# A gate and a depthwise convolution on one core: one product for four taps, other places for the small products, another split of the rows

## Chip, cores and metric

The kernel runs on one core of one Trainium2 chip. The metric is the time on the device in microseconds (us) for one execution; the median of the runs is taken.

## The reference, cut to what matters

The input x has 32 images of 96 channels of 56 x 56 pixels, in fp32. A first layer makes, from image 0, a choice of a 7 x 7 cosine basis for each channel; each image is averaged to 7 x 7 cells, weighted by the basis, mixed over the channels, and gives a gain y. The second layer takes a gain-scaled image, its mean over the pixels, a hidden layer of 24 units, and from it the weights of a depthwise 3 x 3 convolution. The mask keeps four taps: left-up, up, right-up and left.

```
x  = x * y[:, :, None, None] + x                 # y: relu of the mixed, weighted cell means
t  = relu(gamma * (mean(x) @ w1.T - m) * rsqrt(v + eps) + beta)      # 24 units
wt = (t @ w2.T + b2) * MASK                      # 4 live taps per channel
out = depthwise_conv3x3(x, wt) + bias
```

The gain is a factor of each image and channel, so the kernel folds it into the taps, and convolves the x that it loaded.

## The kernel before, in words

The 3,072 planes (image x channel) are 24 tiles of 128 partitions with one plane of 56 x 56 each; three tiles (t = 0, 1, 2) are a group of four images, and there are eight groups g. The taps of a group depend on the cell sums of its own three tiles, so sums run ahead: while tile k is convolved, GpSimd (POOL) folds tile k + 6 in three halvings (`fold_once`, `fold_twice`, `fold_thrice`, L402, L407, L412), and VectorE (DVE) sums the cells of tile k + 5 (`sum_ahead`, L533).

The rows of a tile are split by `ROWS` into three parts, in tiles 0 to 17: 27 rows are D, 18 rows are B, 11 rows are A.
- **A** is the array's part: ScalarE (ACT) seeds a PSUM accumulator with the tap "up" and the bias (`seed_a`), TensorE (PE) adds the other three taps with diagonal matrices in two chunks of rows (`array_taps`), ACT copies it out (`finish_array`, L761).
- **B** is mixed: ACT seeds it (`seed_b`), PE adds two taps in two chunks (`mixed_taps`), DVE adds the last on the way out (`finish_mixed`, L652).
- **D** is DVE's: ACT seeds it (`seed_d`), DVE adds three taps in three instructions (`tap`, L643: LEFT_UP, RIGHT_UP, then LEFT, which writes the result and counts `d_out`).

Every fp32 matmul of the program shows twice in the trace. The accumulators of A, B and D are single: `seed_b` of tile k waits for `finish_mixed` of tile k - 1, `seed_d` waits for LEFT of tile k - 1. The last six tiles (18 to 23, `tail`) have another split with a fourth part for POOL and ACT (`part_rows`, `part`).

Column 0 of D and B has no left neighbours. POOL computes it apart in three instructions (L457, L460, L462) at the start of its step for tile k, before the folds.

Taps of the next group come from a chain of small steps woven into the current group:
1. DVE, tile t = 0: `weigh_cells` (L549, L552, L555) gives `by_image`.
2. PE, tile t = 1: `mix` (L828, L830, twelve records) between the two chunks of A.
3. ACT: `lift_relu` (L706), behind `seed_b` of t = 1, or in the last tiles behind `part`.
4. DVE: `total_step` (L562), between LEFT_UP and RIGHT_UP of t = 1.
5. PE: `hide` (L836) between the chunks of B; ACT: `hidden_relu` (L711), behind `finish_array`; PE: `make_taps` (L842), four products, one for each tap.
6. DVE, tile t = 2: `gained_step` (L567) behind LEFT_UP; PE: `spread_taps` (L849) ahead of B; DVE: `coef_steps` (L574, L579), behind RIGHT_UP.
7. ACT: `diagonals` (L717) and all seeds of t = 0 need the new coefficients.

Each engine has one queue, worked in the order written. SyncE issues all large transfers, nine input and four output buffers: for tile k it waits for B and the edge column, loads tile k + 9, waits for D and A, and stores tile k.

Of the kernel before, what the change touches and what calls it, by code (L numbers as in the profile page):

```python
# [33 lines left out]
ROWS = (27, 18, 11, 0)  # L34
# [84 lines left out]
def build(nc, x, early, narrow, wide, out):  # L119
# [9 lines left out]
    with ExitStack() as ctx:  # L129
# [13 lines left out]
        gate_in = sb("gate_in", [P, E_HID - E_GATE2])  # L143
# [9 lines left out]
        hidden = sb("hidden", [HID, GROUP])  # L153
# [8 lines left out]
        rs_hid = sb("rs_hid", [HID, 1])  # L162
# [4 lines left out]
        a_hid = sb("a_hid", [HID, 1])  # L167
        b_hid = sb("b_hid", [HID, 1])
# [14 lines left out]
        hid_par = early_sb[0:HID, E_HID - E_GATE2:E_END - E_GATE2]  # L183
# [37 lines left out]
        p_hidden = small[0:HID, S_HIDDEN:S_TAPS]  # L221
# [85 lines left out]
        lift_done = sem("lift_done")  # L307
        total_done = sem("total_done")
# [24 lines left out]
        edge_begun = sem("edge_begun")  # L333
        edge_out = sem("edge_out")
# [5 lines left out]
        def _(sp):  # L340
# [22 lines left out]
            for k in range(TILES - 1):  # L363
                sp.wait_ge(b_out, k + 1)
                sp.wait_ge(edge_out, k + 1)
                if k + IN_BUFS < TILES:
                    load(k + IN_BUFS).then_inc(loaded[k % IN_BUFS], 16)
# [21 lines left out]
        def _(pool):  # L389
            eng = nc.gpsimd  # L390
            eng.memset(gate_w[:, :, :], 0.0).then_inc(gate_zeroed, 1)
            eng.memset(expo[:, :], -0.5).then_inc(expo_set, 1)
            pool.wait_ge(expo_set, 1)
# [3 lines left out]
            eng.tensor_tensor(rs_hid[:, :], b_hid[:, :], expo[0:HID, 0:1], ALU.pow).then_inc(rsqrt_done, 1)  # L397
# [49 lines left out]

            for k in range(TILES):
                pool.wait_ge(coef_done, k // PER + 1)
                pool.wait_ge(pad_zeroed, 1)  # L450
                if k >= OUT_BUFS:
                    pool.wait_ge(stored[k % OUT_BUFS], 16 * (k // OUT_BUFS))
                pool.wait_ge(loaded[k % IN_BUFS], 16 * (k // IN_BUFS + 1))
                n = top_a(k)
                rows = grid(k)[:, 0:n, 0:2]
                each = coef[:, k // PER % 2, k % PER, UP:RIGHT_UP + 1].rearrange("p (r c) -> p r c", r=1)
                eng.tensor_tensor(edges[:, 0:2, 0:n].rearrange("p c r -> p r c"), rows, each.broadcast_to([P, n, 2]),  # L457
                                  ALU.mult).then_inc(edge_begun, 1)
# [5 lines left out]
                if tail(k):  # L464
                    part_rows(k)
# [218 lines left out]
        def _(act):  # L684
# [85 lines left out]
            for k in range(TILES):  # L770
                g, t = k // PER, k % PER
                seed_b(k)
                if tail(k):
                    part(k)
                if t == 1 and g + 1 < NGROUP:
                    lift_relu(g + 1)
# [198 lines left out]
```

## Time and profile before

| what | value |
|---|---|
| median of 3 runs | 220.35 us (218.67 to 220.83) |
| the profiled execution's own time | 220.57 us |
| its span, first to last instruction | 218.5 us |
| TensorE | 196.0 us busy, 90% |
| VectorE | 193.4 us busy, 89% |
| ScalarE | 134.8 us busy, 62% |
| GpSimd | 172.6 us busy, 79% |
| the chain that ended last | PE 47%, DVE 34%, ACT 7% |

Busy shares are means over a start (to about 36 us), a steady stretch and a tail (from about 173 us). The chain that ended last follows each instruction back to what released it.

### The profile page before, as it was taken

Reading aid. Unit: us, or ns where it says so; the run is one execution under the profiler, and the core shown is the slowest. Engines: PE = TensorE matmul, PEld = TensorE weight load, DVE = VectorE, ACT = ScalarE, POOL = GpSimd, SP = SyncE. Lnnn points to the kernel's source line nnn. Section 1 sums busy time; section 2 is a strip of 40 time slices with the busy share of each in tenths; the row PEclk is TensorE's granted clock in tenths of the full one; section 3 lists DMA queues with packets and bytes.
Section 4 is the critical chain, followed back from the end, with each engine's and each line's share of the span. In section 5 each row is a group of like instructions: output and inputs, shape, how many; then the busy total and the mean of one; then the engine's idle time right before and its main releaser. Section 6 shows DMA issues by size and latency. Waiting matters only on the chain.

```text
span 218.5 us, 2505 instructions
## 1 busy us (share of the span) xinstructions
PE 196.0 (90%) x742; PEld 120.5 (55%) x742; DVE 193.4 (89%) x223; ACT 134.8 (62%) x208; POOL 172.6 (79%) x169
## 2 busy tenths in 40 slices
PE   7382875999999999999999999999999999899990
PEld 3041464675666566657655764675556656665550
DVE  6137958999999999999999999999999997989992
ACT  2001115367585768576867687577658796989960
POOL 4005149799999999999999999999999996696870
PEclk9888555899999999999999999999999999999999
DMA  4999999939999999999999999999999475446677
GB/s 104 262 429 402 441 427 432 417 111 344 425 413 395 413 418 420 427 423 423 430 425 423 439 425 425 430 434 417 432 432 386 188 298 220 184 184 294 294 293 296
DMA packets 8157, 79.07 MB, mean 362 GB/s; under 512 B 1040, under 2 KB 1072, under 8 KB 2128
## 3 DMA queue, kind: packets, MB, share of 16 engines
q1 hardware_dynamic: 8144, 78.92, 88.3%
q8 instruction: 5, 0.08, 0.1%
q14 instruction: 8, 0.07, 0.1%
HBM read 40.38 MB, written 38.54 MB: 361 GB/s over the span
## 4 chain that ended last, share of the span: by engine, by line
PE 47%; DVE 34%; ACT 7%; issue 5%; DMA 3%; SPq 1%; DVEq 1%; ACTq 0%
PE banks L857 33%; DVE banks L643 17%; DVE xout L643 7%; ACT banks L722 4%; DVE xout L652 3%; DMA xout<-x 3%; PE banks L805 3%; PE banks L842 2%; PE banks L828 2%; PE banks L849 2%; PE banks L830 2%; PE banks L792 1%; DVE stats L533 1%; DVE sums L552 1%; DVE stats L520 1%
## 5 line engine op out<-in xcount | busy, mean ns | idle before, releaser
L857 PE MATMUL banks<-xin,diag 128*128 128x330 f32 (+4 forms) x480 | 158.7, 483 | 2.8 <-ACT banks L722 2.7
L857 PEld LDWEIGHTS banks<-xin,diag 128*128 128x128 f32 x480 | 89.2, 193 | 54.8 <-issue 36.3
L722 ACT ACTIVATE banks<-xin,wide_sb,coef 128x616 f32<-128x616 f32 (+4 forms) x77 | 84.8, 1119 | 17.0 <-DVE xout L652 10.2
L402 POOL TENSOR_TENSOR halves<-xin 128x1568 f32<-128x1568 f32 (+2 forms) x22 | 74.0, 3368 | 22.9 <-DVE count L592 13.6
L643 DVE SCALAR_TENSOR_TENSOR banks<-xin,coef,banks 128x1485 f32<-128x1485 f32 (+2 forms) x48 | 82.9, 1727 | 1.6 <-ACT banks L722 0.4
L643 DVE SCALAR_TENSOR_TENSOR xout<-xin,coef,banks 128x1485 f32<-128x1485 f32 (+4 forms) x31 | 42.1, 1377 | 0.9 <-issue 0.3
L407 POOL TENSOR_TENSOR halves<-halves 128x784 f32<-128x784 f32 x18 | 33.3, 1849 | 1.4
L652 DVE SCALAR_TENSOR_TENSOR xout<-xin,coef,banks 128x990 f32<-128x990 f32 (+1 forms) x24 | 29.1, 1212 | 1.7 <-PE banks L857 1.6
L717 ACT ACTIVATE diag<-wide_sb,coef 128x128 f32<-128x128 f32 x72 | 23.4, 389 | 10.5 <-DVE coef L579 10.5
L761 ACT ACTIVATE xout<-banks 128x616 f32<-128x616 f32 (+2 forms) x24 | 15.8, 656 | 15.4 <-PE banks L857 14.8
L412 POOL TENSOR_TENSOR rows<-halves 128x392 f32<-128x392 f32 x18 | 18.3, 1017 | 1.4
L520 DVE TENSOR_REDUCE stats<-xin 128x14 f32<-128x896 f32 (+3 forms) x9 | 11.0, 1227 | 7.8 <-DMA xin<-x 7.8
L533 DVE TENSOR_REDUCE stats<-rows 128x49 f32<-128x392 f32 x18 | 10.0, 555 | 0.0
L439 POOL TENSOR_TENSOR xout<-xout,halves 128x385 f32<-128x385 f32 (+1 forms) x6 | 5.4, 908 | 5.6 <-ACT xout L722 5.6
L842 PEld LDWEIGHTS banks<-hidden,narrow_sb 32*96 32x96 f32 x64 | 6.6, 173 | 5.5 <-issue 5.0
L691 ACT ACTIVATE banks<-banks,b_gate,a_gate 128x784 f32<-128x784 f32 x1 | 1.0, 977 | 13.7 <-PE banks L805 13.7
L435 POOL TENSOR_TENSOR halves<-xin,coef 128x385 f32<-128x385 f32 (+1 forms) x12 | 9.3, 798 | 0.0
L805 PE MATMUL banks<-xout,gate_w 128*128 128x392 f32 x12 | 5.7, 637 | 3.7 <-DMA xout<-x 3.7
L457 POOL TENSOR_TENSOR edges<-xin,coef 128x90 f32<-128x90 f32 (+2 forms) x24 | 8.4, 348 | 0.0
L828 PEld LDWEIGHTS banks<-by_image,wide_sb 128*96 128x96 f32 x48 | 5.2, 178 | 5.5 <-DVE by_image L555 4.1
L460 POOL TENSOR_TENSOR edges<-edges 128x45 f32<-128x45 f32 (+2 forms) x24 | 6.7, 277 | 1.9
L849 PEld LDWEIGHTS banks<-taps,wide_sb 96*128 96x128 f32 x48 | 7.0, 208 | 1.9 <-ACT banks L722 1.0
(79 smaller groups left out, 115.1 us busy)
## 6 DMA issues: line engine op xcount, KB each, us to landing
xin<-x SPq DMA_DIRECT2D x23, 1568.0 KB, 10.4
out<-xout SPq DMA_DIRECT2D x23, 1568.0 KB, 12.6
xout<-x SPq DMA_DIRECT2D x4, 294.0 KB, 5.2
xin<-x SPq DMA_DIRECT2D x1, 1120.0 KB, 14.7
out<-xout SPq DMA_DIRECT2D x1, 700.0 KB, 3.3
wide_sb<-wide SPq DMA_DIRECT2D x1, 499.5 KB, 16.0
xin<-x SPq DMA_DIRECT2D x1, 448.0 KB, 15.3
out<-xout SPq DMA_DIRECT2D x1, 448.0 KB, 3.4
```

What stands on the lines that cost most here:

```text
L402: eng.tensor_tensor(halves[:, j % 2, 0:end, :], cells[:, :, 0, :], cells[:, :, 1, :], ALU.add).then_inc(once_folded, 1)
L407: eng.tensor_tensor(cells[:, :, 0, :], cells[:, :, 0, :], cells[:, :, 1, :], ALU.add).then_inc(twice_folded, 1)
L412: eng.tensor_tensor(rows8[:, j % 2, :].rearrange("p (a f) -> p a f", a=DCT), cells[:, :, 0, :], cells[:, :, 1, :], ALU.add).then_inc(thric ...
L520: return vec.tensor_reduce(cells_of(j, first, end), xin[:, j % IN_BUFS, PAD + first * BLK * W:PAD + end * BLK * W].rearrange("p (a b c d) ...
L533: return vec.tensor_reduce(stats[:, 0, j % PER, :], rows8[:, j % 2, :].rearrange("p (c d) -> p c d", d=BLK), AX.X, ALU.add)
L643: return vec.scalar_tensor_tensor(out=to, in0=grid(k)[:, irows, cols], scalar=weight(k, which), in1=acc, op0=ALU.mult, op1=ALU.add)
L652: vec.scalar_tensor_tensor(out=result(k)[:, top_b(k):top_a(k), ocols], in0=grid(k)[:, irows, cols], scalar=weight(k, LEFT), in1=acc_b(k).r ...
L717: ins = sca.activation(diag[:, k % 2, which, :], ident, ACT.Copy, scale=weight(k, which))
L722: return sca.activation(acc, above_rows(k, first, end), ACT.Identity, bias=bias[:, k % PER:k % PER + 1], scale=weight(k, UP))
L761: sca.activation(xout[:, k % OUT_BUFS, top_a(k) * W:top_p(k) * W], acc_a(k), ACT.Copy).then_inc(a_out, 1)
L805: ins = mm(gate_out[:, part], gate_w[:, t, :], image0[:, t, part], start=(t == 0), stop=(t == PER - 1))
L857: return mm(to, diag[:, k % 2, which, :], grid(k)[:, irows, cols], start=False, stop=(which == LEFT), skip_group_check=True)
```

## The change

- `ROWS` is 27/17/12 in place of 27/18/11: one row of each of tiles 0 to 17 goes from B to A.
- The hidden layer's product has its weights four times side by side, so its 32 rows appear in four blocks of partitions. `hidden_relu` is four instructions, one for each block, into a block-diagonal tile zeroed once, and `make_taps` is one product over 128 rows in place of four over 32. Parameters of the hidden layer are laid on 128 partitions; five copies on ScalarE at the start make the wider weights.
- ScalarE's order: `lift_relu` stands ahead of `part`, `hidden_relu` behind `diagonals`.
- `mix` stands behind the second chunk of A.
- In tiles 0 to 17 the edge column is two instructions on ScalarE (`edge_products`, behind `seed_b` and `lift_relu`) and one on POOL (`edge_sum`, behind the folds). The last six tiles keep POOL's three. The load of tile k + 9 waits for ScalarE's two and not for the edge column's end.

The sizes of `gate_in`, `rs_hid`, `a_hid`, `b_hid`, `p_hidden`, new semaphores and the zeroing of `hidden` on POOL are left out of the diff.

```diff
@@ -31,7 +31,7 @@
 
 
 
-ROWS = (27, 18, 11, 0)
+ROWS = (27, 17, 12, 0)
 TAIL_ROWS = (24, 16, 9, 7)
 LAST_ROWS = (25, 16, 10, 5)
 AHEAD_FOLD = 6
...
@@ -150,7 +150,9 @@
         by_image = sb("by_image", [P, 2, PER, GROUP])
         lift = sb("lift", [C, GROUP])
         total = sb("total", [C, GROUP])
-        hidden = sb("hidden", [HID, GROUP])
+        hidden = sb("hidden", [P, TAPS, GROUP])
+        w_hid4 = sb("w_hid4", [C, TAPS, HID])
+        w_tap4 = sb("w_tap4", [P, C])
         taps = sb("taps", [C, TAPS, GROUP])
         spread = sb("spread", [P, PER * TAPS, GROUP])
         coef = sb("coef", [P, 2, PER, TAPS])
...
@@ -362,9 +368,10 @@
 
             for k in range(TILES - 1):
                 sp.wait_ge(b_out, k + 1)
+                if k + IN_BUFS < TILES:
+                    sp.wait_ge(edge_scaled, 2 * k + 2)
+                    load(k + IN_BUFS).then_inc(loaded[k % IN_BUFS], 16)
                 sp.wait_ge(edge_out, k + 1)
-                if k + IN_BUFS < TILES:
-                    load(k + IN_BUFS).then_inc(loaded[k % IN_BUFS], 16)
                 sp.wait_ge(d_out, k + 1)
                 sp.wait_ge(a_out, k + 1)
                 if tail(k):
...
@@ -445,23 +453,35 @@
                 pool.wait_ge(part_step, 2 * n + 2)
                 eng.tensor_tensor(to, to, scaled, ALU.add).then_inc(part_out, 1)
 
+            def edge_rows(k):
+
+                pool.wait_ge(coef_done, k // PER + 1)
+                pool.wait_ge(edge_out, k)
+                pool.wait_ge(pad_zeroed, 1)
+                pool.wait_ge(stored[k % OUT_BUFS], 16 * (k // OUT_BUFS))
+                pool.wait_ge(loaded[k % IN_BUFS], 16 * (k // IN_BUFS + 1))
+                m = top_a(k)
+                n = k - (TILES - AHEAD_FOLD)
+                rows = grid(k)[:, 0:m, 0:2]
+                each = coef[:, k // PER % 2, k % PER, UP:RIGHT_UP + 1].rearrange("p (r c) -> p r c", r=1)
+                eng.tensor_tensor(edges[:, 0:2, 0:m].rearrange("p c r -> p r c"), rows, each.broadcast_to([P, m, 2]),
+                                  ALU.mult).then_inc(edge_begun, 1)
+                pool.wait_ge(edge_begun, 2 * n + 1)
+                eng.tensor_tensor(edges[:, 2, 0:m], edges[:, 0, 0:m], edges[:, 1, 0:m], ALU.add).then_inc(edge_begun, 1)
+                pool.wait_ge(edge_begun, 2 * n + 2)
+                eng.tensor_tensor(result(k)[:, 0:m, 0], edges[:, 2, 0:m],
+                                  bias[:, k % PER:k % PER + 1].broadcast_to([P, m]), ALU.add).then_inc(edge_out, 1)
+
+            def edge_sum(k):
+
+                n = top_a(k)
+                pool.wait_ge(edge_scaled, 2 * k + 2)
+                eng.tensor_tensor(result(k)[:, 0:n, 0], result(k)[:, 0:n, 0], edges[:, k % 2, 0:n],
+                                  ALU.add).then_inc(edge_out, 1)
+
             for k in range(TILES):
-                pool.wait_ge(coef_done, k // PER + 1)
-                pool.wait_ge(pad_zeroed, 1)
-                if k >= OUT_BUFS:
-                    pool.wait_ge(stored[k % OUT_BUFS], 16 * (k // OUT_BUFS))
-                pool.wait_ge(loaded[k % IN_BUFS], 16 * (k // IN_BUFS + 1))
-                n = top_a(k)
-                rows = grid(k)[:, 0:n, 0:2]
-                each = coef[:, k // PER % 2, k % PER, UP:RIGHT_UP + 1].rearrange("p (r c) -> p r c", r=1)
-                eng.tensor_tensor(edges[:, 0:2, 0:n].rearrange("p c r -> p r c"), rows, each.broadcast_to([P, n, 2]),
-                                  ALU.mult).then_inc(edge_begun, 1)
-                pool.wait_ge(edge_begun, 2 * k + 1)
-                eng.tensor_tensor(edges[:, 2, 0:n], edges[:, 0, 0:n], edges[:, 1, 0:n], ALU.add).then_inc(edge_begun, 1)
-                pool.wait_ge(edge_begun, 2 * k + 2)
-                eng.tensor_tensor(result(k)[:, 0:n, 0], edges[:, 2, 0:n],
-                                  bias[:, k % PER:k % PER + 1].broadcast_to([P, n]), ALU.add).then_inc(edge_out, 1)
                 if tail(k):
+                    edge_rows(k)
                     part_rows(k)
                 j = k + AHEAD + 1
                 if j < TILES:
@@ -472,6 +492,8 @@
                     fold_twice(j)
                     pool.wait_ge(twice_folded, j - AHEAD)
                     fold_thrice(j)
+                if not tail(k):
+                    edge_sum(k)
 
 
         @block.vector
...
@@ -693,6 +715,9 @@
             act.wait_ge(gate2_mm, 1)
             sca.activation(gate_act[:, :], p_gate2, ACT.Tanh, bias=gate_par[0:NF, 4:5],
                            scale=1.0 / HW).then_inc(gate_tanh, 1)
+            act.wait_ge(narrow_in, 16)
+            for which in range(TAPS):
+                sca.activation(w_tap4[HID * which:HID * (which + 1), :], w_tap[:, which, :], ACT.Copy).then_inc(w_tap_copied, 1)
             act.wait_ge(chosen_done, 1)
             sca.activation(chosen_rows[:, :, :, :],
                            chosen[:, :, :].rearrange("p t (j q) -> p t j q", j=1).broadcast_to([NF, PER, GROUP, QUAD]),
@@ -700,6 +725,9 @@
             act.wait_ge(wide_in, 16)
             act.wait_ge(filt_mm, 1)
             sca.activation(p_mask, image_of, ACT.Copy).then_inc(mask_set, 1)
+            sca.activation(w_hid4[:, :, :], w_hid.rearrange("p (k h) -> p k h", k=1).broadcast_to([C, TAPS, HID]),
+                           ACT.Copy).then_inc(w_hid_copied, 1)
+            act.wait_ge(hidden_zeroed, 1)
 
             def lift_relu(g):
                 act.wait_ge(total_mm, g + 1)
@@ -708,8 +736,10 @@
 
             def hidden_relu(g):
                 act.wait_ge(hidden_mm, g + 1)
-                sca.activation(hidden[:, :], p_hidden, ACT.Relu, bias=b_hid[:, :],
-                               scale=a_hid[:, :]).then_inc(hidden_done, 1)
+                for which in range(TAPS):
+                    rows = slice(HID * which, HID * (which + 1))
+                    sca.activation(hidden[rows, which, :], p_hidden[rows, :], ACT.Relu, bias=b_hid[rows, :],
+                                   scale=a_hid[rows, :]).then_inc(hidden_done, 1)
 
             def diagonals(k):
                 act.wait_ge(coef_done, k // PER + 1)
@@ -721,6 +751,18 @@
                 act.wait_ge(loaded[k % IN_BUFS], 16 * (k // IN_BUFS + 1))
                 return sca.activation(acc, above_rows(k, first, end), ACT.Identity, bias=bias[:, k % PER:k % PER + 1],
                                       scale=weight(k, UP))
+
+            def edge_products(k):
+
+                n = top_a(k)
+                if k >= OUT_BUFS:
+                    act.wait_ge(stored[k % OUT_BUFS], 16 * (k // OUT_BUFS))
+                sca.activation(result(k)[:, 0:n, 0], grid(k)[:, 0:n, 0], ACT.Identity,
+                               bias=bias[:, k % PER:k % PER + 1], scale=weight(k, UP)).then_inc(edge_scaled, 1)
+                if k >= 2:
+                    act.wait_ge(edge_out, k - 1)
+                sca.activation(edges[:, k % 2, 0:n], grid(k)[:, 0:n, 1], ACT.Copy,
+                               scale=weight(k, RIGHT_UP)).then_inc(edge_scaled, 1)
 
             def seed_a(k):
                 if k > 0:
@@ -770,15 +812,18 @@
             for k in range(TILES):
                 g, t = k // PER, k % PER
                 seed_b(k)
+                if t == 1 and g + 1 < NGROUP:
+                    lift_relu(g + 1)
                 if tail(k):
                     part(k)
-                if t == 1 and g + 1 < NGROUP:
-                    lift_relu(g + 1)
+                else:
+                    edge_products(k)
                 finish_array(k)
+                if k + 1 < TILES:
+                    diagonals(k + 1)
                 if t == 1 and g + 1 < NGROUP:
                     hidden_relu(g + 1)
                 if k + 1 < TILES:
-                    diagonals(k + 1)
                     seed_a(k + 1)
                     seed_d(k + 1)
 
@@ -833,14 +878,18 @@
             def hide(g):
 
                 pe.wait_ge(total_done, g + 1)
-                mm(p_hidden, w_hid, total[:, :], start=True, stop=True).then_inc(hidden_mm, 1)
+                if g == 0:
+                    pe.wait_ge(w_hid_copied, 1)
+                mm(p_hidden, w_hid4[:, :, :].rearrange("p k h -> p (k h)"), total[:, :],
+                   start=True, stop=True).then_inc(hidden_mm, 1)
 
             def make_taps(g):
 
-                pe.wait_ge(hidden_done, g + 1)
-                for which in range(TAPS):
-                    ins = mm(p_taps[:, which, :], w_tap[:, which, :], hidden[:, :], start=True, stop=True)
-                ins.then_inc(taps_mm, 1)
+                if g == 0:
+                    pe.wait_ge(w_tap_copied, TAPS)
+                pe.wait_ge(hidden_done, TAPS * (g + 1))
+                mm(p_taps.rearrange("p k n -> p (k n)"), w_tap4[:, :], hidden[:, :, :].rearrange("p k n -> p (k n)"),
+                   start=True, stop=True).then_inc(taps_mm, 1)
 
             def spread_taps(g):
 
@@ -880,9 +929,9 @@
                 pe.wait_ge(diag_done, k + 1)
                 pe.wait_ge(seeded_a, k + 1)
                 array_taps(k, 0)
+                array_taps(k, 1).then_inc(conv_a, 1)
                 if t == 1 and ahead:
                     mix(g + 1)
-                array_taps(k, 1).then_inc(conv_a, 1)
                 pe.wait_ge(seeded_b, k + 1)
                 if t == 2 and ahead:
                     spread_taps(g + 1)
```

## Rows read from the trace of the kernel before

**Rows 1.** Windows by engine, one steady group: length, busy us (instructions), clock, DMA share, GB/s.
```profile
105.80:128.30 22.50, 22.40 (x89) 13.69 (x88) 21.92 (x23) 15.96 (x24) 21.56 (x19) 1.00 1.01 429
```
**Rows 2.** Timeline, VectorE: start us, length us, engine, line, operation, count, idle before.
```profile
101.15 0.16 DVE L567 SCALAR_TENSOR_TENSOR taps<-lift,banks 96x16 f32<-96x16 f32 x1
...
103.19 0.20 DVE L579 TENSOR_REDUCE coef<-spread 128x12 f32<-128x48 f32 x1
...
105.79 1.25 DVE L652 SCALAR_TENSOR_TENSOR xout<-xin,coef,banks 128x990 f32<-128x990 f32 x1 [0.26 <-PE banks L857]
...
113.66 0.18 DVE L555 TENSOR_TENSOR by_image<-sums,banks 128x24 f32<-128x24 f32 x1
...
116.58 0.15 DVE L562 SCALAR_TENSOR_TENSOR total<-lift,banks 96x4 f32<-96x4 f32 x1
...
118.52 1.76 DVE L643 SCALAR_TENSOR_TENSOR xout<-xin,coef,banks 128x1485 f32<-128x1485 f32 x1
...
121.98 1.77 DVE L643 SCALAR_TENSOR_TENSOR banks<-xin,coef,banks 128x1485 f32<-128x1485 f32 x1
...
123.65 0.16 DVE L567 SCALAR_TENSOR_TENSOR taps<-lift,banks 96x16 f32<-96x16 f32 x1
```
**Rows 3.** The same timeline, TensorE's products.
```profile
101.60 0.74 PE L849 MATMUL banks<-taps,wide_sb 96*128 96x16 f32 x6
...
102.19 11.61 PE L857 MATMUL banks<-xin,diag 128*128 128x495 f32 x34
...
113.89 0.67 PE L828 MATMUL banks<-by_image,wide_sb 128*96 128x4 f32 x6
...
114.42 0.65 PE L830 MATMUL banks<-by_image,wide_sb 128*96 128x4 f32 x6
...
118.16 0.22 PE L836 MATMUL banks<-total,wide_sb 96*32 96x4 f32 x2
...
120.17 0.84 PE L842 MATMUL banks<-hidden,narrow_sb 32*96 32x4 f32 x8
```
**Rows 4.** The same timeline, ScalarE.
```profile
104.32 2.40 ACT L722 ACTIVATE banks<-xin,wide_sb,coef 128x616 f32<-128x616 f32 x2
...
116.16 0.34 ACT L706 ACTIVATE lift<-banks,b_chan,a_chan 96x4 f32<-96x4 f32 x1
...
116.61 0.68 ACT L761 ACTIVATE xout<-banks 128x616 f32<-128x616 f32 x1
...
118.42 0.35 ACT L711 ACTIVATE hidden<-banks,b_hid,a_hid 32x4 f32<-32x4 f32 x1 [1.13 <-PE banks L836]
...
118.68 0.97 ACT L717 ACTIVATE diag<-wide_sb,coef 128x128 f32<-128x128 f32 x3
...
119.56 3.58 ACT L722 ACTIVATE banks<-xin,wide_sb,coef 128x616 f32<-128x616 f32 x3
```
**Rows 5.** Timeline of POOL, two of its instructions.
```profile
106.44 0.35 POOL L457 TENSOR_TENSOR edges<-xin,coef 128x90 f32<-128x90 f32 x1
...
107.45 3.54 POOL L402 TENSOR_TENSOR halves<-xin 128x1568 f32<-128x1568 f32 x1
```
**Rows 6.** Timelines of PE and DVE, the first group's chain.
```profile
46.46 0.59 PE L828 MATMUL banks<-by_image,wide_sb 128*96 128x4 f32 x6
...
48.70 0.15 DVE L562 SCALAR_TENSOR_TENSOR total<-lift,banks 96x4 f32<-96x4 f32 x1
...
54.47 1.77 DVE L643 SCALAR_TENSOR_TENSOR banks<-xin,coef,banks 128x1485 f32<-128x1485 f32 x1 [0.44 <-ACT banks L722]
```
**Rows 7.** Timelines of ACT and DVE, the last group's chain.
```profile
184.57 0.57 ACT L761 ACTIVATE xout<-banks 128x504 f32<-128x504 f32 x1
185.27 0.35 ACT L711 ACTIVATE hidden<-banks,b_hid,a_hid 32x4 f32<-32x4 f32 x1
...
188.14 2.14 ACT L722 ACTIVATE banks<-xin,wide_sb,coef 128x840 f32<-128x840 f32 x2 [0.21 <-DVE xout L643]
...
184.70 0.15 DVE L562 SCALAR_TENSOR_TENSOR total<-lift,banks 96x4 f32<-96x4 f32 x1 [1.04 <-ACT lift L706]
```

More of the change, by code:

```diff
@@ L142, in build @@
         gate_w = sb("gate_w", [P, PER, P])
-        gate_in = sb("gate_in", [P, E_HID - E_GATE2])
+        gate_in = sb("gate_in", [P, E_END - E_GATE2])
         early_sb = sb("early_sb", [C, E_END - E_GATE2])
@@ L161, in build @@
         rs_gate = sb("rs_gate", [P, 1])
-        rs_hid = sb("rs_hid", [HID, 1])
+        rs_hid = sb("rs_hid", [P, 1])
         a_chan = sb("a_chan", [C, 1])
@@ L166, in build @@
         b_gate = sb("b_gate", [P, 1])
-        a_hid = sb("a_hid", [HID, 1])
-        b_hid = sb("b_hid", [HID, 1])
+        a_hid = sb("a_hid", [P, 1])
+        b_hid = sb("b_hid", [P, 1])
         gate_sum = sb("gate_sum", [P, 1])
@@ L182, in build @@
         chan_par = early_sb[:, E_CHAN - E_GATE2:E_GATE - E_GATE2]
-        hid_par = early_sb[0:HID, E_HID - E_GATE2:E_END - E_GATE2]
+        hid_par = gate_in[:, E_HID - E_GATE2:E_END - E_GATE2]
         ones = narrow_sb[:, N_ONES:N_SHIFT]
@@ L220, in build @@
         p_total = small[0:C, S_TOTAL:S_HIDDEN]
-        p_hidden = small[0:HID, S_HIDDEN:S_TAPS]
+        p_hidden = small[:, S_HIDDEN:S_TAPS]
         p_taps = small[0:C, S_TAPS:S_SPREAD].rearrange("p (k n) -> p k n", k=TAPS)
@@ L307, in build @@
         lift_done = sem("lift_done")
+        w_hid_copied = sem("w_hid_copied")
+        w_tap_copied = sem("w_tap_copied")
+        hidden_zeroed = sem("hidden_zeroed")
         total_done = sem("total_done")
@@ L333, in build @@
         edge_begun = sem("edge_begun")
+        edge_scaled = sem("edge_scaled")
         edge_out = sem("edge_out")
@@ L392, in _ @@
             eng.memset(expo[:, :], -0.5).then_inc(expo_set, 1)
+            eng.memset(hidden[:, :, :], 0.0).then_inc(hidden_zeroed, 1)
             pool.wait_ge(expo_set, 1)
@@ L396, in _ @@
             eng.tensor_tensor(rs_chan[:, :], b_chan[:, :], expo[0:C, :], ALU.pow).then_inc(rsqrt_done, 1)
-            eng.tensor_tensor(rs_hid[:, :], b_hid[:, :], expo[0:HID, 0:1], ALU.pow).then_inc(rsqrt_done, 1)
+            eng.tensor_tensor(rs_hid[:, :], b_hid[:, :], expo[:, 0:1], ALU.pow).then_inc(rsqrt_done, 1)
             def fold_once(j, end=DCT):
@@ L484, in _ @@
             for j in range(GROUP):
-                vec.tensor_copy(gate_in[QUAD * j:QUAD * (j + 1), :], early_sb[0:NF, 0:E_HID - E_GATE2]).then_inc(gate_copied, 1)
+                vec.tensor_copy(gate_in[QUAD * j:QUAD * (j + 1), :], early_sb[0:NF, :]).then_inc(gate_copied, 1)
             vec.tensor_scalar(b_chan[:, :], chan_par[:, 4:5], EPS, None, ALU.add).then_inc(fold, 1)
+            dve.wait_ge(gate_copied, GROUP)
             vec.tensor_scalar(b_hid[:, :], hid_par[:, 3:4], EPS, None, ALU.add).then_inc(fold, 1)
-            dve.wait_ge(gate_copied, GROUP)
             vec.tensor_scalar(b_gate[:, :], gate_par[:, 3:4], EPS, None, ALU.add).then_inc(fold, 1)
```

## The prediction, made before the changed kernel ran

> **What bounds the kernel now.** I read the page's busy shares, then windows over single groups of three tiles, then the timeline of one group engine by engine, then the waits. The steady stretch repeats every 22.50 us, and in it three engines and the transfers are nearly full: PE 22.40, DVE 21.92, POOL 21.56 us, DMA share 1.01 at 429 GB/s; only ACT (15.96) has room [rows 1]. The reader is to see that nobody has a large wait, so what counts is the cycle of hand-overs in which one group's taps are made. Let G be the end of `gained_step`, 101.31 (101.15 and 0.16) [rows 2]. PE then spreads the taps and works 34 records without a gap (B of t=2, A and B of t=0, the first chunk of A of t=1) until 113.80, and `mix` starts at 113.89, 0.05 after `by_image` ends at 113.84 [rows 2, 3]. `mix` ends at 115.07. ACT takes the lift at 116.16, because `seed_b` held it, and DVE starts `total_step` at 116.58, directly behind its tap. So between the end of `mix` and the lift there is 1.09 us of slack, and DVE waits for nothing there [rows 2 to 4]. DVE's only wait in a group is 0.26 us, for PE, ahead of `finish_mixed` of t=2 [rows 2]. Its own work would thus make 22.24.
>
> **Rows 27/17/12.** B has two taps on PE, A three. Per tile PE has 2 x (4 x 495 + 3 x 330 + 3 x 275) = 7,590 columns, afterwards 2 x (2 x 495 + 2 x 440 + 6 x 330) = 7,700. The block of 34 records has 13,530 columns in 11.61 us, 0.858 ns each [rows 3]; 110 more are 0.09 us a tile, 0.28 a group. DVE's `finish_mixed` loses 55 of 990 elements, 0.06 us a tile. At t=2, though, the first tap waits for `seed_d` and not for `finish_mixed`: it starts at 121.98, 1.70 after LEFT ended at 120.28, which is ACT's `seed_d` (about 1.6) and two hand-overs [rows 2, 4]. There the 0.06 is worth nothing.
>
> **One product for four taps.** `make_taps` takes 0.77 of PE (120.17 to the next product at 120.94) and becomes one pair, about 0.20 like a pair of `spread_taps` (0.59 for three pairs). `hide` has 128 columns of weights for 32, some 0.05 more [rows 3]. PE's own work falls to 22.40 + 0.28 - 0.57 + 0.05 = 22.16 a group. But both products stand behind `mix`, in a part of the cycle where PE isn't last. The price is on ACT: `hidden_relu` is four instructions. One occupies ACT for 0.26 (118.42 to 118.68) [rows 4]. The trace has no such followers; they lie between 0.19 (a diagonal takes 0.29 and has 128 columns, 0.11 us at the seeds' pace) and 0.35 (its whole length). I take 0.25, nearest to the row of the same shape.
>
> **Mix behind A's second chunk.** This is the costly step. From G: spreading starts 0.05 later, now that PE comes earlier (it was 0.29), and takes 0.59: G+0.64. B of t=2, 3,740 columns, 3.21: 3.85. A of t=0 needs its seed: coefficients end at G+2.08 and `seed_a` started at G+3.01 [rows 2, 4]; with 0.85 and 0.06 for its new row it ends at 3.92, and A starts at 3.96. A, B and now both chunks of A, 11,660 columns, 10.00: 13.96. Then 0.09 and `mix` 1.18: 15.23. Lift 0.05 and 0.34, hand-over 0.08: `total_step` starts at G+15.70. Before it started at G+15.27. DVE, which has shed its 0.26 wait and 0.06, now stands idle there, and behind it wait RIGHT_UP, LEFT, the sum, `finish_mixed` and the next `gained_step`: 7.23 us that nothing shortens. The cycle becomes 22.9, and I take **0.40 us more a group**. Bounds: without the late seed and at 0.833 ns a column (two cycles at the granted 1.00, 2.4 GHz) 0.2; above, with a late ScalarE, 0.8 (below).
>
> **Edges, and the order on ScalarE.** POOL gives up 1.01 us a tile (106.44 to 107.45) [rows 5] and gets back one instruction of 0.3 and a gap. Nothing waited for POOL: its edge column is ready at 107.45, and the store that needs it waits for the tile's B, one tile later, so this is worth nothing. Moved behind the folds it ends about 6.5 us later, still some 2.5 us ahead of B's end. SyncE's queue is not delayed: load of k+9 waits for ACT's two, done while B is still in the array. ACT gains 0.5 us a tile. It has 6.5 us idle in a group [rows 1], most of it at t=0 and t=2, where it waits for A, LEFT and the coefficients; that covers four of the six. At t=1, between lift and `seed_d`, it now has lift 0.25, edges 0.50, copy 0.68, diagonals 0.88, hidden 1.00, `seed_a` 0.86: 4.17 behind a lift at G+15.28, so 19.45; DVE's LEFT ends at 15.70 + 3.70 = 19.40 and a hand-over later `seed_d` could start. Just in time, without reserve. If the cover is gone, every 0.05 us on the six small instructions is 0.3 us a group.
>
> **Start and tail.** In the first group `mix` starts at 46.46 with PE behind [rows 6]; 2,090 more columns make 1.79 us, and `total_step` comes at 49.87 for 48.70. Of these 1.17 us the 0.44 that the next tile waited for ACT takes up its part: +0.8. Ahead of it, four hidden instructions (+0.7) and a shorter `make_taps` (-0.9 at the low clock) cancel. The new copies lie in ACT's idle time. In the last group DVE waited 1.04 us for a lift behind `part` [rows 7]; that goes. But ACT ran full from there to `seed_d` with 0.21 idle: three more hidden instructions (0.75) meet 0.21 and a pause of 0.2 ahead of the hidden one, so the next tile starts 0.2 to 0.4 later all the same. I take +0.2.
>
> **Sum.** 0.8 + 5 x 0.40 + 0.2 = +3.0 us. The profiled execution, 220.57 with a span of 218.5, would become 223.6, its span 221.5; it lies 0.2 above the median of 220.35, so **223.4** for the median.
>
> **Rivals.**
> - *DVE sets the pace* (not slower). If PE came to the end of `mix` 0.6 us earlier than I reckon, `total_step` would not wait and DVE's own cycle decides: 22.50 less 0.12 (the 0.26 wait, of which `seed_d` of t=0 gives back the rest) and 0.06 = 22.32. For it: PE sheds 0.24 a group. Against: that is shed behind `mix`, and PE waits for `gained_step`, so it can't be carried on. The point: `mix` ended by G+14.7. Price -0.9 over five groups, the tail near zero: 219.4; with all of the 1.04 kept, 218.4. The transfers allow it, barely: 429 GB/s now [rows 1]. The Trainium skill, "DMA: Bandwidth & Descriptors", section "Where 436 GB/s comes from", puts the ceiling of the ports at 435.2 GB/s, which for 9.63 MB is 22.13 us a group. By that rule no engine's relief is worth over 0.4 us a group, or about 218; the trace agrees in that no steady window shows more than 429.
> - *The chunk costs half* (within 1%). Seeds on time and small hand-overs: 0.2 a group, 0.6 at the start: +1.7, 222.0.
> - *ScalarE late as well* (slower still). Small instructions at 0.30: seven of them add 0.35, `seed_d` of t=2 is late: 0.75 a group, tail 0.5: +5.0, 225.4.
> - That POOL's relief or the combined product does not come about would change nothing, as neither is on the cycle.
>
> **Chances.** Forecast's case 0.50 (222.6 to 224.3), ScalarE late 0.12, half cost 0.22, DVE's pace 0.16. About 1%, 2.2 us, is what a measurement here can tell from no change. Slower by over 1% takes the first two: 0.62. Within 1% has the half cost and most of DVE's pace: 0.31; faster 0.07, where the tail's 1.04 is kept too. Range 220.3 to 225.0: it leaves out most of DVE's pace and the upper part of the late ScalarE.
>
> **What would show it.** `total_step` with an idle time of 0.4 to 0.6 us released by ACT's lift in each steady group; `finish_mixed` without its wait; TensorE waiting for `gained_step` ahead of spreading; groups 22.9 apart; POOL with some 0.6 us idle a tile; ACT without idle time between lift and `seed_d` of t=1. I am wrong if groups are under 22.5 apart, or if DVE's longest wait is for `seed_d`.

## The result, and the profile after

The changed kernel takes 227.12 us (median of 4 runs, 226.25 to 228.42) beside 220.59 for the kernel before: 1.031 times, 95% interval 1.027 to 1.036. The forecast was 223.4 with a range to 225.0. The direction was right and the amount was half of what came. Medians here and below are over all executions, while the ratios leave out those that ran over 1.5% above the fastest of their kernel, at a lower granted clock, so the two need not have the same order. The profiled execution has a span of 224.2 us, 5.7 more than before.

Busy times of two groups, each from one `gained_step` to the next. Columns are length, busy us with instructions for PE, PE's weight loads, DVE, ACT and POOL, then granted clock, DMA share and GB/s:

```profile
81.19:104.43 23.24, 22.11 (x83) 13.31 (x82) 21.88 (x24) 19.05 (x33) 20.03 (x13) 1.00 1.01 415
104.43:127.65 23.22, 22.09 (x83) 13.31 (x82) 21.86 (x23) 19.02 (x33) 19.98 (x13) 1.00 1.01 413
```

Against [rows 1] the group is 0.73 us longer, though PE, DVE and POOL all have less to do. Only ACT has more: 19.0 for 16.0 us. No engine is full any more. The DMA share still reads 1.01, but it did so at 429 GB/s too, and in the steady stretch no engine waits for a transfer. So this is a cycle of waits, and the busy column can't show it.

Where the 5.7 us lie, read from the starts of `gained_step` on DVE (the seven after the first one):

```profile
57.97 0.16 DVE L589 SCALAR_TENSOR_TENSOR taps<-lift,banks 96x16 f32<-96x16 f32 x1
81.19 0.16 DVE L589 SCALAR_TENSOR_TENSOR taps<-lift,banks 96x16 f32<-96x16 f32 x1
104.43 0.16 DVE L589 SCALAR_TENSOR_TENSOR taps<-lift,banks 96x16 f32<-96x16 f32 x1
127.65 0.16 DVE L589 SCALAR_TENSOR_TENSOR taps<-lift,banks 96x16 f32<-96x16 f32 x1
150.88 0.16 DVE L589 SCALAR_TENSOR_TENSOR taps<-lift,banks 96x16 f32<-96x16 f32 x1
174.11 0.16 DVE L589 SCALAR_TENSOR_TENSOR taps<-lift,banks 96x16 f32<-96x16 f32 x1
196.53 0.16 DVE L589 SCALAR_TENSOR_TENSOR taps<-lift,banks 96x16 f32<-96x16 f32 x1
```

Before, the second of all eight started at 56.14, the seventh at 168.80, the last at 190.74. So +1.83 is there by the second, five groups add 116.14 - 112.66 = 3.48, the sixth (22.42 for 21.94) 0.48, and the end after the last takes 0.1 less.

ScalarE's timeline from B's seed to A's seed of t=2 (start, length, engine, line, operation, count, idle before) answers to [rows 4]:

```profile
118.09 1.15 ACT L752 ACTIVATE banks<-xin,wide_sb,coef 128x952 f32<-128x952 f32 x1 [1.00 <-DVE xout L674]
119.65 0.35 ACT L734 ACTIVATE lift<-banks,b_chan,a_chan 96x4 f32<-96x4 f32 x1 [0.41 <-PE banks L875]
119.91 0.46 ACT L760 ACTIVATE xout<-xin,wide_sb,coef 128x44 f32<-128x44 f32 x1
120.27 0.36 ACT L764 ACTIVATE edges<-xin,coef 128x44 f32<-128x44 f32 x1
120.53 0.71 ACT L803 ACTIVATE xout<-banks 128x672 f32<-128x672 f32 x1
121.14 0.97 ACT L747 ACTIVATE diag<-wide_sb,coef 128x128 f32<-128x128 f32 x3
122.02 1.45 ACT L741 ACTIVATE hidden<-banks,b_hid,a_hid 32x4 f32<-32x4 f32 x4
123.49 3.52 ACT L752 ACTIVATE banks<-xin,wide_sb,coef 128x672 f32<-128x672 f32 x3
```

From the lift to the seed of A ACT has no idle time that counts (0.03 us ahead of each relu but the first, and ahead of the seed). The four relus take 1.47 us to the next start, 0.37 each. One took 0.26 before. PE's timeline of the same group answers to [rows 3]:

```profile
101.32 3.57 PE L906 MATMUL banks<-xin,diag 128*128 128x330 f32 x12 [0.69 <-ACT banks L752]
104.73 0.81 PE L898 MATMUL banks<-taps,wide_sb 96*128 96x16 f32 x6
105.39 13.28 PE L906 MATMUL banks<-xin,diag 128*128 128x495 f32 x40
118.51 0.59 PE L873 MATMUL banks<-by_image,wide_sb 128*96 128x4 f32 x6
...
123.52 0.34 PE L891 MATMUL banks<-hidden,w_tap 128*96 128x16 f32 x2 [0.44 <-ACT hidden L741]
124.55 3.57 PE L906 MATMUL banks<-xin,diag 128*128 128x330 f32 x12 [0.69 <-ACT banks L752]
```

PE waits 0.44 for the relus and 0.69 for A's seed of t=2. These rows close a circle: A of t=2 at 101.32, spreading, B, A, B, A, `mix` until 119.61, lift, edges, copy, diagonals, four relus, A's seed, and A of t=2 again at 124.55. That is 18.3 us of PE and 4.9 of ACT, 23.23 together, in which the views show no wait. DVE stands beside it, with two waits that answer to [rows 2]:

```profile
120.03 0.15 DVE L584 SCALAR_TENSOR_TENSOR total<-lift,banks 96x4 f32<-96x4 f32 x1 [0.30 <-ACT lift L734]
...
125.98 1.77 DVE L665 SCALAR_TENSOR_TENSOR banks<-xin,coef,banks 128x1485 f32<-128x1485 f32 x1 [0.74 <-ACT banks L752]
```

The first is the one I forecast. The larger, for `seed_d` of t=2, I had put at nothing; that it would be DVE's longest was my own sign of being wrong.

### The profile page after: what moved, and what is told of

It is laid out like the page before. It is cut to its first block, busy times and chain, and to the rows that moved or that the text cites. A ratio compares the mean times of both kernels' runs of the same rounds, so it can differ in the third digit from the quotient of the medians.

```text
span 224.2 us, 2409 instructions
## 1 busy us (share of the span) xinstructions
PE 193.0 (86%) x694; PEld 117.3 (52%) x694; DVE 192.8 (86%) x223; ACT 156.7 (70%) x273; POOL 163.2 (73%) x134
## 4 chain that ended last, share of the span: by engine, by line
PE 53%; ACT 20%; DVE 14%; issue 6%; DMA 3%; SPq 1%; DVEq 1%; ACTq 0%
PE banks L906 42%; DVE banks L665 8%; ACT banks L752 7%; ACT hidden L741 4%; ACT diag L747 3%; DMA xout<-x 3%; PE banks L850 3%; PE banks L898 2%; DVE xout L665 2%; ACT xout L803 2%; PE banks L875 2%; PE banks L873 2%; PE banks L837 1%; ACT xout L760 1%; DVE stats L542 1%
## 5 line engine op out<-in xcount | busy, mean ns | idle before, releaser
L752 ACT ACTIVATE banks<-xin,wide_sb,coef 128x672 f32<-128x672 f32 (+4 forms) x77 | 84.3, 1119 | 13.0 <-DVE xout L674 7.9
L674 DVE SCALAR_TENSOR_TENSOR xout<-xin,coef,banks 128x935 f32<-128x935 f32 (+1 forms) x24 | 28.0, 1168 | 0.5 <-PE banks L906 0.5
L803 ACT ACTIVATE xout<-banks 128x672 f32<-128x672 f32 (+2 forms) x24 | 16.5, 688 | 7.8 <-PE banks L906 7.8
L741 ACT ACTIVATE hidden<-banks,b_hid,a_hid 32x4 f32<-32x4 f32 x32 | 11.0, 343 | 1.5 <-PE banks L883 0.9
L760 ACT ACTIVATE xout<-xin,wide_sb,coef 128x44 f32<-128x44 f32 x18 | 8.3, 462 | 0.2
L898 PE MATMUL banks<-taps,wide_sb 96*128 96x16 f32 x48 | 7.1, 276 | 0.9 <-DVE taps L589 0.9
L734 ACT ACTIVATE lift<-banks,b_chan,a_chan 96x4 f32<-96x4 f32 x8 | 2.8, 349 | 7.3 <-PE banks L875 7.2
```

The lines of the kernel that those rows point to most:

```text
L674: vec.scalar_tensor_tensor(out=result(k)[:, top_b(k):top_a(k), ocols], in0=grid(k)[:, irows, cols], scalar=weight(k, LEFT), in1=acc_b(k).r ...
L741: sca.activation(hidden[rows, which, :], p_hidden[rows, :], ACT.Relu, bias=b_hid[rows, :], scale=a_hid[rows, :]).then_inc(hidden_done, 1)
L752: return sca.activation(acc, above_rows(k, first, end), ACT.Identity, bias=bias[:, k % PER:k % PER + 1], scale=weight(k, UP))
L803: sca.activation(xout[:, k % OUT_BUFS, top_a(k) * W:top_p(k) * W], acc_a(k), ACT.Copy).then_inc(a_out, 1)
L898: ins = mm(p_spread[:, TAPS * t:TAPS * (t + 1), :], to_rows[:, t, :], taps[:, :, :], start=True, stop=True)
```

## The experiments

Ratios are to the kernel before on the same chip, measured along with each. "Group" is the distance of two `gained_step` in the steady stretch, from the profile. A single span is less sure than the group, for a reason told at the end.

| kernel | median us | ratio, interval | group us |
|---|---|---|---|
| changed kernel | 227.12 | 1.031 (1.027 to 1.036) | 23.23 |
| its hidden layer as before | 219.99 | 0.997 (0.993 to 1.001) | 22.60 |
| its mix as before | 226.29 | 1.023 (1.015 to 1.031) | 23.01 |
| its edges as before | 223.81 | 1.016 (1.009 to 1.022) | 22.77 |
| its rows 27/18/11 | 224.19 | 1.016 (1.010 to 1.023) | 22.86 |
| hidden layer and mix as before | 220.48 | 0.999 (0.995 to 1.002) | 22.62 |
| before, with the new hidden layer alone | 229.63 | 1.040 (1.035 to 1.045) | 23.65 |
| changed, relus on 128 partitions (1 run) | 224.65 | | 22.75 |
| changed, relus all on partitions 0 to 31 (1 run) | 223.87 | | 22.69 |
| changed, one relu | 220.90 | 1.003 (0.998 to 1.007) | 22.60 |
| before, ScalarE's order alone | 219.50 | 0.997 (0.992 to 1.002) | 22.50 |
| the same and edges on ScalarE | 219.78 | 0.993 (0.989 to 0.997) | 22.51 |
| the same and one product by one relu | 219.11 | 0.996 (0.991 to 1.001) | 22.42 |

Theory: ScalarE's row from lift to A's seed, above all the four relus, sets the cycle. Rival: the late `mix`, which was the step of my forecast.

**1. The hidden layer put back**

```diff
-                for which in range(TAPS):
-                    rows = slice(HID * which, HID * (which + 1))
-                    sca.activation(hidden[rows, which, :], p_hidden[rows, :], ...)
+                sca.activation(hidden[:, :], p_hidden, ACT.Relu, bias=b_hid[:, :], scale=a_hid[:, :])
...
+                for which in range(TAPS):
+                    ins = mm(p_taps[:, which, :], w_tap[:, which, :], hidden[:, :], start=True, stop=True)
```

> The changed kernel with the hidden layer of before: one relu on 32 partitions, four products for four taps. Theory (ScalarE's queue): the groups are 23.23 us apart because lift, two edge products, copy, diagonals, four hidden relus and the seed of A stand in a row between the end of mix and A of t=2; the four relus occupy 1.47 us of it, one would occupy 0.37 or less, so 1.1 us leaves this row, and the next cycle takes over, the one of gained_step, mix and total_step at 22.5 to 22.7. 0.6 x 5 groups, 0.6 at the start, 0.5 in the tail: 4 us faster than the changed kernel, about 223. Rival (the late mix, the step of my forecast): DVE waits for the lift because mix comes late, and the hidden relus stand behind that, so nothing moves: 226 to 227.5.

219.99 us: the whole loss is gone, 7.1 us, and the group is 22.60, inside the theory's 22.5 to 22.7. The total is 3 us below the 223 I expected: between the two profiled spans, which differ by 5.1, the five groups make 3.13 where I had 3.0, but the last group 1.26 where I had 0.5. Without this part nothing of the loss is left. The rival falls, since `mix` is as late as ever here. The next cycle is not surely the one I named: PE is busy for all 22.60 us of this group (experiment 6 goes on from there). The 0.3 wait that the late `mix` causes is still to be seen:

```profile
118.07 0.15 DVE L581 SCALAR_TENSOR_TENSOR total<-lift,banks 96x4 f32<-96x4 f32 x1 [0.30 <-ACT lift L725]
```

**2. Mix back between A's chunks**

```diff
                 array_taps(k, 0)
-                array_taps(k, 1).then_inc(conv_a, 1)
                 if t == 1 and ahead:
                     mix(g + 1)
+                array_taps(k, 1).then_inc(conv_a, 1)
```

> The changed kernel with mix back between the chunks of A. ScalarE's queue: lift can start only 0.45 us earlier (seed_b then ends last), so ScalarE's row is 0.45 shorter and groups are about 22.75 apart: 2.5 us faster than the changed kernel, 224.5; DVE loses its 0.3 wait at total_step but keeps most of its wait for seed_d. Late mix: all of the loss comes back, groups at 22.5 or below: 221.

23.01, half of the expected gain, and 226.29 us where I expected 224.5. The lift is earlier, directly behind `seed_b`, and DVE's 0.3 wait is gone; but `hide` now stands behind A's second chunk, and the relus wait 0.15 for it:

```profile
119.95 0.34 ACT L734 ACTIVATE lift<-banks,b_chan,a_chan 96x4 f32<-96x4 f32 x1
...
122.55 1.46 ACT L741 ACTIVATE hidden<-banks,b_hid,a_hid 32x4 f32<-32x4 f32 x4 [0.15 <-PE banks L883]
```

**3. Edges back on POOL** (three instructions of POOL for each tile, none on ScalarE)

```diff
-                else:
-                    edge_products(k)
...
-                if tail(k):
-                    edge_rows(k)
+                edge_rows(k)
```

> The changed kernel with the edge column on POOL as before. ScalarE's queue: 0.62 us leaves the row between lift and the seed of A: groups at 22.65, 2.8 us faster than the changed kernel, 224.2, unless POOL, full again at 7.5 us a tile, holds something back. Late mix: edges stand behind the lift and don't matter: 226 to 227.5.

22.77, 0.46 less a group of the 0.62 that left the row; 223.81. The rest of the 0.62 went into a short pause ahead of the relus, which now wait for `hide`: diagonals started at 96.74 and took 0.88, the relus started at 97.76. POOL, full again, held nothing back.

**4. Rows 27/18/11 in the changed kernel**

```diff
-ROWS = (27, 17, 12, 0)
+ROWS = (27, 18, 11, 0)
```

> The changed kernel with 27/18/11 rows. Both theories: PE has 550 columns less between the seed of A of t=2 and the end of mix, 0.47 us, and ScalarE 0.1 less. ScalarE's queue: groups 22.65 to 22.9, 1.7 to 2.8 us faster, 224.3 to 225.4. Late mix: only the 220 columns between gained_step and mix count, 0.2 a group, 1 us faster, 226.

22.86, inside the interval of the theory; the rival's 0.2 is too little. Experiments 1 to 4 take 0.63, 0.22, 0.46 and 0.37 off one and the same cycle, 1.68 together and more than the 0.73 that it is too long. So the gains of single parts can't be added: another cycle of nearly the same length takes over.

**5. The new hidden layer alone, in the kernel before** (the edit of 1 the other way round, on the kernel before)

> The kernel before with the new hidden layer alone: four relus, one product for four taps; rows, mix, edges and ScalarE's order as before. ScalarE's queue: there the relus start at 118.42 in the group shown and stand ahead of diagonals, seed of A and seed of D; 1.1 to 1.2 us more puts the seed of D of t=2 that much later, DVE waits for it once a group, and its 0.26 wait for PE goes: groups 23.2 to 23.4 apart for 22.50, +0.9 x 6 = 5 to 6 us, 226. Rival (it is the sum of the parts that fills ScalarE): without edges ScalarE has idle time enough, PE's shorter make_taps shows: 219 to 221.

The worst of all, 229.63 us where I expected 226, and +1.15 a group where I expected 0.7 to 0.9: that is about the 1.1 to 1.2 us of three more relus, and no help from anywhere. Without the new order they even stand ahead of the diagonals:

```profile
100.60 1.46 ACT L725 ACTIVATE hidden<-banks,b_hid,a_hid 32x4 f32<-32x4 f32 x4 [1.10 <-PE banks L852]
102.08 0.98 ACT L731 ACTIVATE diag<-wide_sb,coef 128x128 f32<-128x128 f32 x3
...
105.40 1.77 DVE L649 SCALAR_TENSOR_TENSOR banks<-xin,coef,banks 128x1485 f32<-128x1485 f32 x1 [1.29 <-ACT banks L736]
```

So it is not the sum of the parts that fills ScalarE; the full change, with edges and late `mix` on top, is 0.4 us a group better than this. Its new order of ScalarE is the likely reason, but no run puts that order alone on this kernel.

**6. Hidden layer and mix put back together** (the edits of 1 and 2)

> The changed kernel with hidden layer and mix of before, so rows 27/17/12, edges and ScalarE's order are what is left of the change. ScalarE's queue: lift and seed of A are early enough; PE, full at 22.6 us a group with four products, sets the pace: 219.5 to 220, as with the hidden layer alone put back. Late mix: DVE's 0.3 wait at total_step goes and groups fall by 0.1 to 0.3: 218.5 to 219.5.

22.62 for 22.60, and 220.48 us. With four small products PE is full, 23.00 of 23.00 us busy from 90 to 113 us, and where `mix` stands is then worth nothing.

**7 and 8. Why 0.37 and not 0.25.** The four relus on all 128 partitions, and all four on partitions 0 to 31:

```diff
-                    sca.activation(hidden[rows, which, :], p_hidden[rows, :], ACT.Relu, bias=b_hid[rows, :],
+                    sca.activation(hidden[:, which, :], p_hidden[:, :], ACT.Relu, bias=b_hid[:, :],
```

```diff
-                    rows = slice(HID * which, HID * (which + 1))
+                    rows = slice(0, HID)
```

> The changed kernel with each of the four hidden relus on all 128 partitions (it fills the off-diagonal blocks too, so taps are wrong). In the changed kernel the four start 0.37 us apart, while one on 32 partitions in the kernel before gives way to its follower after 0.26. If it is the change of the partitions from one to the next that costs, they start 0.24 to 0.27 apart here, the row is 0.45 shorter and groups are 22.8 apart. If it is four small reads of PSUM in a row, 0.37 and 23.2.

> The changed kernel with all four hidden relus on partitions 0 to 31 (three blocks are left out, so taps are wrong). Change of partitions: 0.24 to 0.27 apart, groups 22.8. Small reads of PSUM in a row: 0.37, groups 23.2.

ScalarE's rows, 128 partitions first, then partitions 0 to 31, each with the seed that follows:

```profile
122.31 1.08 ACT L740 ACTIVATE hidden<-banks,b_hid,a_hid 128x4 f32<-128x4 f32 x4
123.27 3.54 ACT L751 ACTIVATE banks<-xin,wide_sb,coef 128x672 f32<-128x672 f32 x3
```

```profile
121.78 1.05 ACT L741 ACTIVATE hidden<-banks,b_hid,a_hid 32x4 f32<-32x4 f32 x4
122.73 3.50 ACT L752 ACTIVATE banks<-xin,wide_sb,coef 128x672 f32<-128x672 f32 x3
```

0.96 and 0.95 us for four, 0.24 each. One instruction is as long as before (0.35 and 0.33, beside 0.33 to 0.35); what is lost when each begins at another partition than the one before it is the overlap of about 0.1 us. That the ranges differ is not enough: the seed covers all 128 partitions and still starts 0.24 behind a relu on partitions 0 to 31. In the changed kernel even the first relu, on partitions 0 to 31, has its follower on 32 to 63 only 0.36 behind it. And the four copies at the start, which all read partitions 0 to 31 and write to 0, 32, 64 and 96, don't overlap either: at lengths of 0.27 to 0.28 they start 0.29 to 0.31 apart. So it seems enough that what is written begins at another partition (changed kernel):

```profile
17.68 1.18 ACT L720 ACTIVATE w_tap<-narrow_sb 32x96 f32<-32x96 f32 x4
```

Groups are 22.75 and 22.69. So with the relus at the price I had put in, the group is still 0.2 us longer than before, and ScalarE's row still ends it, as the kernel with all relus on partitions 0 to 31 shows:

```profile
123.77 3.57 PE L906 MATMUL banks<-xin,diag 128*128 128x330 f32 x12 [0.55 <-ACT banks L752]
125.19 1.77 DVE L665 SCALAR_TENSOR_TENSOR banks<-xin,coef,banks 128x1485 f32<-128x1485 f32 x1 [0.20 <-ACT banks L752]
```

**9. One relu.** The changed kernel keeps its one product for four taps, but the blocks off the diagonal are made by PE:

```diff
+                mm(p_hidden, ident, away, start=True, stop=False)     # away: 0 on the diagonal blocks, else -2^30
                 mm(p_hidden, w_hid4[:, :, :].rearrange("p k h -> p (k h)"),
-                   total[:, :],
-                   start=True, stop=True).then_inc(hidden_mm, 1)
+                   total[:, :].rearrange("p (k n) -> p k n", k=1).broadcast_to([C, TAPS, GROUP]),
+                   start=False, stop=True).then_inc(hidden_mm, 1)
...
-                for which in range(TAPS):
-                    ...
+                sca.activation(hidden[:, :, :], p_hidden, ACT.Relu, bias=b_hid[:, :], scale=a_hid[:, :])
```

(It rests on a positive scale of every hidden unit; the constant unit that carries the taps' bias gets the scale of a unit weight for it.)

> The changed kernel, but the off-diagonal blocks are pushed far below zero by one more product into the hidden layer's accumulator (unit matrix times a constant of 0 and -2^30), so one relu over 128 partitions and 16 columns makes the block-diagonal tile, in 0.25 to 0.3 us of ScalarE instead of 1.47. ScalarE's queue: 1.15 us leaves the row; then the cycle of the late mix decides, 22.5 to 22.6 us a group: 219 to 220.5, as with the hidden layer of before. Rival (it is the wide products, not the relus, that cost): 224 to 227.

220.90 us, 0.4 above my interval, and a group of 22.60. The wide product was never the trouble. Here PE is not full (22.16 of 22.61 us), and the late `mix` is alone as the cycle: PE waits 0.44 for `gained_step`, DVE 0.30 for the lift, and neither waits for a seed.

```profile
102.47 0.81 PE L900 MATMUL banks<-taps,wide_sb 96*128 96x16 f32 x6 [0.44 <-DVE taps L591]
...
117.78 0.15 DVE L586 SCALAR_TENSOR_TENSOR total<-lift,banks 96x4 f32<-96x4 f32 x1 [0.30 <-ACT lift L736]
119.76 0.36 ACT L741 ACTIVATE hidden<-banks,b_hid,a_hid 128x16 f32<-128x16 f32 x1
120.01 0.91 ACT L752 ACTIVATE banks<-xin,wide_sb,coef 128x672 f32<-128x672 f32 x1
```

So with the late `mix` as its cycle the kernel is 0.10 us a group over 22.50, not the 0.40 of the forecast. Against experiment 12, which has the same hidden layer, the late `mix` and rows 27/17/12 together cost 0.18.

**10 to 12. What of the change is worth keeping.** ScalarE's order alone; with the edges; with the one relu and the one product too (the edit of 9). Rows and `mix` are as before in all three.

```diff
                 seed_b(k)
+                if t == 1 and g + 1 < NGROUP:
+                    lift_relu(g + 1)
                 if tail(k):
                     part(k)
-                if t == 1 and g + 1 < NGROUP:
-                    lift_relu(g + 1)
                 finish_array(k)
+                if k + 1 < TILES:
+                    diagonals(k + 1)
                 if t == 1 and g + 1 < NGROUP:
                     hidden_relu(g + 1)
```

> The kernel before with ScalarE's order of the change alone: lift ahead of part, hidden relu behind the diagonals. Groups stay 22.5 apart (PE is full). In the tail DVE's 1.04 wait at total_step goes, ScalarE then has 0.2 us of the pause ahead of the hidden relu back as well: 0.5 to 1.0 us faster, 219.5 to 220. If the tail's chain runs on through ScalarE's seed of D, only 0.2 to 0.4.

> As the kernel with ScalarE's order alone, with the edge column on ScalarE and POOL as in the change. Edges cost nothing with one hidden relu: the same within 0.3 us, groups 22.4 to 22.5. If POOL, full before, had held the groups at 22.5, they fall to 22.3 and it is 1 us faster.

> ScalarE's order and edges of the change, rows 27/18/11 and mix as before, and the one product for four taps, made by the one relu over 16 columns and the extra product. PE sheds 0.57 for make_taps and takes 0.2 for the extra product and 0.05: 22.15 to 22.2 a group; then DVE's own work decides, 22.24, or the seed of D: groups 22.25 to 22.35 apart, 0.15 to 0.25 x 6 = 1 to 1.5 us faster than order and edges without it: 218.3 to 219.

The order alone leaves the groups at 22.50 and shortens the last one from 21.94 to 21.34 us, 0.60; DVE then waits 0.54 for `seed_d` where it had waited 1.04 for the lift:

```profile
188.20 1.60 DVE L659 SCALAR_TENSOR_TENSOR banks<-xin,coef,banks 128x1320 f32<-128x1320 f32 x1 [0.54 <-ACT banks L738]
```

With the edges moved the group stays at 22.51: POOL, now with idle time, had held nothing. The one product by one relu brings the group to 22.42, 0.08 and not the 0.15 to 0.25 expected. PE is now 0.36 us idle in a group ahead of spreading, so it has room; the cycle there goes from `gained_step` over spreading and B of t=2 to `finish_mixed`, which still waits 0.19:

```profile
102.90 0.81 PE L900 MATMUL banks<-taps,wide_sb 96*128 96x16 f32 x6 [0.36 <-DVE taps L591]
...
107.17 1.25 DVE L676 SCALAR_TENSOR_TENSOR xout<-xin,coef,banks 128x990 f32<-128x990 f32 x1 [0.19 <-PE banks L908]
```

The ratios of the table can't rank the three. Executions with a like granted clock, 0.935 or more, have medians of 219.00 us (6, ScalarE's order alone), 219.25 (7, with the edges) and 218.74 (6, with the one product), beside 220.19 (23) of the kernel before: each is about 0.5% faster, and the last, with the shortest group, is probably the best of them.

## Why the prediction was wrong, by its own steps

- **"I take 0.25, nearest to the row of the same shape"** for the four relus. This is the step that failed. They took 0.37 each, 1.47 us for 1.00. The row [rows 4] was of one relu on partitions 0 to 31 with a follower on all partitions; what each of the four meets, a follower that begins at another partition, no row showed. I had its length, 0.35, as the upper bound, and should have priced the four with it. Experiments 7 and 8 show what the step was worth: with relus at 0.24 the group falls from 23.23 to 22.75 and 22.69, 0.5 of the 0.73 us, and the single executions took 224.65 and 223.87 us, near the forecast of 223.4.
- **"Two edge products 0.50".** They took 0.62, of which the first 0.36 and the second 0.26. The first has a scale and a bias for each partition, the second only a scale. The Trainium skill, "ScalarE: Activation LUTs", section "What ACT_TABLE_LOAD costs", says that each such operand adds about 93 ns and that followers overlap by about as much. The trace agrees in both for the edges: their lengths, 0.46 and 0.36, differ by 0.10, and each follower starts 0.10 before the end. An estimate from that page's figures for two such operands and four columns is 0.38, and 0.28 to the next start; the relus were 0.33 to 0.35 long, and their followers started after 0.37.
- **"4.17 behind a lift at G+15.28 ... Just in time, without reserve."** With both corrections the lift was followed by A's seed after 3.84 us and not 3.31. My own sentence "if the cover is gone, every 0.05 us on the six small instructions is 0.3 us a group" was right: 0.53 us too little on the row, and no reserve. And I checked the row only against DVE. PE needed A's seed at the same time (0.69 wait), which closed a cycle of PE and ACT alone; it waited 0.55 even with relus at 0.24.
- **"0.40 us more a group" for the late mix.** The mechanism is real, as experiment 9 shows, but in the changed kernel it didn't set the pace, and its size was wrong: as the only cycle it makes 0.10. There `total_step` starts at 117.78, 15.45 behind G (102.33) and not 15.70, and from it to the end of the next `gained_step` (124.93) are 7.15 us, not 7.23. The seed that I thought late at A of t=0 did not interrupt PE's 40 records, and `mix` took 1.11 (116.25 to 117.36), not 1.18: small terms, most of them on the side of more, summed to 0.3. This error and that of the relus went opposite ways, so the forecast's total was nearer than its steps.
- **Start, +0.8.** It was 1.83. At the low clock the four relus cost 1.2 us more than the one before (I had 0.7) and the wide hidden product 0.3 (I had nothing), against 1.0 saved in `make_taps`: `gained_step` came 0.81 later, where I had 0, of which 0.25 was there at the first lift already. The second group, 25.04 for 24.02, added 1.0 for the 0.8 I had.
- **Tail, +0.2.** It was 0.48: the relus again. `seed_d` came so late that DVE waited 1.80 there; the 1.04 for the lift was gone as foreseen.

```profile
195.02 1.60 DVE L665 SCALAR_TENSOR_TENSOR banks<-xin,coef,banks 128x1320 f32<-128x1320 f32 x1 [1.80 <-ACT banks L752]
```

- **The rival "ScalarE late as well"** had the mechanism in the main, and the group: 0.75, measured 0.73. That the number fits so well is partly luck: it counted 0.35 more on ScalarE's row, which had 0.53 more, on top of a late `mix` that was worth less, and it saw only `seed_d`, not PE's wait for A's seed. It got a chance of 0.12, because I held the margin for zero and not for negative. Its total, 225.4, was still 1.7 short, mostly at the start.
- **The signs.** TensorE was to wait for `gained_step` ahead of spreading; it didn't, it waited for the relus and for A's seed. `total_step` waited 0.30 and not 0.4 to 0.6, groups were 23.23 apart and not 22.9, and POOL was idle for 1.1 us a tile and not 0.6. My sentence that no steady window shows more than 429 GB/s holds for windows of a whole group; in slices of 5.5 us the profile's page has up to 439 in the steady stretch.
- Right were: edges at t=0 and t=2 hidden, POOL's relief worth nothing, SyncE not delayed, PE's sum (22.1 busy for 22.16), a wait at `total_step`, `finish_mixed` without a wait, ACT without idle time between lift and `seed_d`.

In short, the sum is 1.83 (start) + 3.48 (five groups) + 0.48 (last group) - 0.1 (end) = 5.7 against 0.8 + 2.0 + 0.2.

## What to carry to other kernels

A change that takes work off a full engine may pay for it with small instructions on another. Price each of these by the time from its start to the next start, add up the whole row of instructions in which they stand, and compare its end with every engine that waits for it, not with one. When a margin comes out at zero and its terms can hardly shrink, the case behind it deserves more than a small chance. Four relus on four blocks of partitions can be one over all of them, if the array first pushes the unwanted blocks below zero (1.47 us became 0.25).

## What the runs showed of the hardware

- ScalarE's instructions overlap by about 0.1 us with their follower, but here not when the follower begins at another partition: 0.36 to 0.37 from start to start on four blocks of 32, 0.24 on one block or on all 128, at lengths of 0.33 to 0.36. The seed of A, on all partitions, started 0.37 behind the fourth relu (partitions 96 to 127), but 0.24 behind one on partitions 0 to 31. Copies that read the same partitions and wrote to others lost it too. Whether anything but the first partition matters, and the cause inside the engine, are open.
- TensorE's clock rises from 1.2 to 2.4 GHz at the start, at a time that differs between profiles. In the kernel of experiment 6 PE had worked without a pause since 35.67 us, and the granted clock was 0.89 at 38 to 40 us; in that of experiment 1 it had done so since 35.81, and the clock was still 0.50 at 40 to 42 and 1.00 at 42 to 44. In the window 40 to 42 it was 0.90 in the kernel before and 0.81 in the changed one. It was 0.50 there in the profiles of experiments 11 and 12 too, whose spans, 220.1 and 219.0, are above the 218.5 of the kernel before though their groups are no longer. With one profile of each kernel, how much of a span this moves is not measured; executions of the kernel of experiment 12 took 218.66 to 219.14 us at a mean clock of 0.940 to 0.957, and 221.08 to 221.38 at 0.926.
